# One gated decoder layer on one core: slot attention in one block with its weights loaded ahead, the last expert's down weights in pieces, and token attention written out with scores two batches ahead

## The reference, cut to what matters

```python
x = x + tanh(g_xattn) * cross_attention_and_feed_forward(layernorm(x), ctx)   # not changed
y = layernorm(x)                                                              # [8, 512, 512]
q = broadcast(slot_query)                                                     # [8, 16, 512]
o = q + mha(q, y, y, d_W*, d_b*)                                              # slot attention
h = layernorm(o) * e_ln_g + e_ln_b
u = silu(h @ e_W1 + e_b1) ; g = silu(h @ e_Wg + e_bg)                         # expert e takes slot e
o = o + (u * g) @ e_W2 + e_b2                                                 # 16 experts
x = x + tanh(g_ffn) * mha(y, o, o, c_W*, c_b*)                                # token attention
```

## Time and profile before

| | us |
|---|---|
| median of 3 runs | 2560.3 (2555.49 to 2560.6) |
| the profiled execution | 2563.1 |
| its span | 2561.3 |
| mean granted TensorE clock, share of full speed | 0.929 |
| feed forward ends | 1741.5 |
| slot attention ends | 1934.8 |
| experts end | 2388 |
| last vector step ends | 2556.5 |

### The profile page before, as it was taken

The page is one execution under the profiler, slowest core; times in us unless marked ns, Lnnn a source line. Parts: engine busy times, 40 slices in busy tenths (PEclk is TensorE's granted clock), DMA queues, the critical chain, the costliest instruction groups (busy, mean ns, idle before and its releaser), DMA issues. The chain is left out here.

```text
span 2561.3 us, 29863 instructions
## 1 busy us (share of the span) xinstructions
PE 2231.3 (87%) x11583; PEld 1677.0 (65%) x11583; DVE 959.9 (37%) x1566; ACT 630.7 (25%) x974; POOL 384.4 (15%) x237
## 2 busy tenths in 40 slices
PE   7999999999699999999999999997887535455787
PEld 5677777776588888888888888885773112121576
DVE  7656566655322222222222233334541000000577
ACT  2544455446211111111111111112320000000221
POOL 5443344423100000000000000001210000000022
PEclk9899999999899999999999999997997768777798
DMA  4122210211433333333334353314659999999365
GB/s 148 70 88 88 88 55 34 88 66 34 165 137 137 135 141 137 139 137 136 144 143 143 143 192 124 127 66 159 234 215 394 429 427 429 432 422 424 141 262 213
DMA packets 109716, 466.50 MB, mean 182 GB/s; under 512 B 10850, under 2 KB 12418, under 8 KB 82980
## 3 DMA queue, kind: packets, MB, share of 16 engines
q1 hardware_dynamic: 100372, 406.45, 41.5%
q10 hardware_dynamic: 9264, 58.99, 5.6%
HBM read 381.52 MB, written 83.89 MB: 182 GB/s over the span
## 5 line engine op out<-in xcount | busy, mean ns | idle before, releaser
L1177 ACT ACTIVATE ff_sig<-ff_gate 128x512 f32<-128x512 f32 x128 | 76.5, 598 | 744.7 <-PE ff_a L1137 744.7
L1215 DVE TENSOR_TENSOR u<-ff_sig,ff_a 128x512 f32<-128x512 f32 x128 | 88.0, 687 | 452.3 <-ACT ff_sig L1177 452.3
L1818 PE MATMUL e_down<-e_w,e_ug 128*32 128x512 f32 x512 | 78.0, 765 | 192.0 <-DMA e_w<-in_L_ffn_e_W 186.1
L1137 PE MATMUL ff_gate<-ff_nT_hi,w_hi 128*128 128x512 f32 x512 | 200.3, 391 | 15.1 <-DMA ff_nT_lo<-xnT 15.1
L1137 PE MATMUL ff_gate<-ff_nT_lo,w_hi 128*128 128x512 f32 x512 | 200.0, 391 | 0.0
L1137 PE MATMUL ff_gate<-ff_nT_hi,w_lo 128*128 128x512 f32 x512 | 199.9, 390 | 0.0
L1137 PE MATMUL ff_a<-ff_nT_lo,w_hi 128*128 128x512 f32 x512 | 199.2, 389 | 0.0
L1137 PE MATMUL ff_a<-ff_nT_hi,w_hi 128*128 128x512 f32 x512 | 199.2, 389 | 0.0
L1137 PE MATMUL ff_a<-ff_nT_hi,w_lo 128*128 128x512 f32 x512 | 199.2, 389 | 0.0
L1151 PE MATMUL ff_down<-w_hi,u_hi 128*128 128x512 f32 x512 | 199.2, 389 | 0.0
L1151 PE MATMUL ff_down<-w_lo,u_hi 128*128 128x512 f32 x512 | 199.2, 389 | 0.0
(11 more groups left out here) (365 smaller groups left out, 4457.5 us busy)
## 6 DMA issues: line engine op xcount, KB each, us to landing
e_w<-in_L_ffn_e_W SPq DMA_DIRECT2D x17, 4096.0 KB, 24.4
e_wg<-in_L_ffn_e_Wg SPq DMA_DIRECT2D x16, 4096.0 KB, 34.3
e_w<-in_L_ffn_e_W ACTq DMA_DIRECT2D x14, 4096.0 KB, 49.5
ff_nT_hi<-xnT SPq DMA_DIRECT2D x32, 1024.0 KB, 4.8
ff_nT_lo<-xnT SPq DMA_DIRECT2D x32, 1024.0 KB, 6.8
ff_x<-x SPq DMA_DIRECT2D x32, 1024.0 KB, 8.0
x<-ff_x SPq DMA_DIRECT2D x32, 1024.0 KB, 4.4
ff_raw<-in_L_xattn_Wff SPq DMA_DIRECT2D x36, 256.0 KB, 5.6
```

The source lines that it names most:

```text
L1137: last = nc.tensor.matmul(UP[f % 2][g][:, :], w, m_, start=c == 0, stop=c == 3 * KT - 1)
L1177: nc.scalar.activation(sig[:, f % 2, :], UP[f % 2][1][:, :], ACT.Silu).then_inc(sig_ready, 1)
L1215: nc.vector.tensor_tensor(u32[:, f % 2, :], sig[:, f % 2, :], UP[f % 2][0][:, :], ALU.mult).then_inc(u_ready, 1)
L1818: last = nc.tensor.matmul(YB[q * QW:(q + 1) * QW, :], ug[:, j * Q + q, :], w2[i][:, q * J + j, :], start=j == 0, stop=j == J - 1)
```

## The change

The slot stage becomes one block in which every batch is written out. The order on PE becomes: turn y of b, turn z of b-2, turn the probabilities of b-1, scores of b, sums of b-1. q is made with Wq as the stationary side, 16 columns at a time, into columns, so it isn't turned; A is made of q itself, on four row groups of PE (64 instructions of 16 columns), and q_diag serves the shift alone. The slot queries and column biases, and the first rows of x, are loaded at the end of feed forward; the 17 small rows are loaded behind the store of yT and of batch 0. The value and output products follow in the same block.

```diff
+                        load_slot(sp, 0)
                     with sp.Fori(0, PAIRS - 1) as pair:
                         step(q, pair, pair + 1)
+                    if q == Q - 1:
+                        load_slot(sp, 1)
...
+                for c in range(KT):
+                    for k in range(KT):
+                        last = nc.tensor.matmul(G[5][:, c * NS:(c + 1) * NS], wq[:, k, c * P:(c + 1) * P], sqT[:, k, :], start=k == 0, stop=k == KT - 1)
...
+                for c in range(KT):
+                    for k in range(KT):
+                        for g in range(CH):
+                            rows = slice(g * SD, (g + 1) * SD)
+                            at = (k * KT + c) * NS
+                            last = nc.tensor.matmul(G[g][:, at:at + NS], wkT[rows, c, k * P:(k + 1) * P], qT[rows, c, :], start=True, stop=True)
...
-                with pe.Fori(1, B) as b:
+                for b in range(B):
                     turn_rows(b)
-                    turn_probs(b)
+                    if b >= 2:
+                        turn_sums(b - 2)
+                    if b >= 1:
+                        turn_probs(b - 1)
                     score(b)
-                    sums(b, b - 1)
-                pe.drain().then_inc(g_ready, U_P)
-                turn_probs(B)
-                sums(B, B - 1)
+                    if b >= 1:
+                        sums(b - 1)
+                turn_sums(B - 2)
+                turn_probs(B - 1)
+                sums(B - 1)
+                turn_sums(B - 1)
```

```diff
                 sp.wait_ge(g_ready, E - 1)
+                sp.dma_start(lent[:, 0, :, :], c_weight("q")).then_inc(wq_in, 16)
...
+                sp.wait_ge(last_w2_in[Q - 2], 16)
+                sp.dma_start(lent[:, 1, :, :], c_weight("k")).then_inc(wk_in, 16)
...
                 def finish(e, i):
-                    shrink(e, i)
+                    pe.wait_ge(wq_in, 16)
+                    for c in range(KT):
+                        for k in range(KT):
+                            last = nc.tensor.transpose(WB[c][:, k * P:(k + 1) * P], lent[:, 0, k, c * P:(c + 1) * P], ident[:, :])
...
+                    for q in range(Q):
+                        pe.wait_ge(last_w2_in[q], 16)
+                        for j in range(J):
+                            last = nc.tensor.matmul(YB[q * QW:(q + 1) * QW, :], ug[:, j * Q + q, :], w2[i][:, q * J + j, :], start=j == 0, stop=j == J - 1)
+                    last.then_inc(down_ready, 1)
                     add_parts(e)
```

```diff
+                            if first:
+                                nc.tensor.matmul(bank[at:at + CH * NS, :], first_head[0:1, :], bo, start=False, stop=True)
...
+                for b in range(3):
+                    values(b)
+                pe.wait_ge(w_free, dve_done["wk", KT - 1, CH - 1])
+                scores(0)
+                for b in range(3, 5):
+                    values(b)
+                scores(1)
+                for b in range(5, B):
+                    values(b)
+                for b in range(B - 2):
+                    turn(b)
+                    scores(b + 2)
+                    sums(b)
+                turn(B - 2)
+                turn(B - 1)
+                sums(B - 2)
+                sums(B - 1)
```

998 lines of the change are left out of this document (532 added, 466 removed).

## The result

The changed kernel took 2532.2 us (median of 4 runs, 2528.0 to 2536.3), the kernel before 2559.3 in the same comparison: a ratio of 0.9897, 95% interval 0.9874 to 0.9919, so 1.0% faster, 27 us. The forecast was 2523 with a range of 2505 to 2541. The profiled execution took 2528.0 us, its span 2526.2; before, it was 2563.1 and 2561.3, a difference of 35.1.

What follows compares the result with a forecast made beforehand. TensorE paces slot attention, the weight stream the experts; token attention is mixed. Gains of 21.4 (slots) and 16.1 (token stage, expert's 4.4 loss paid) make 37.5 us: 2525.6 profiled, 2523 median; own range 2513 to 2532, 8-in-10 range 2505 to 2541.

Steps and rivals of the forecast that it cites:

- Entry to batch 1: Slot stage up to batch 1's scores: quicker q and A, earlier yT store; gain 6 us, from 3 to 9.
- Six regular batches: Slot stage: turning z a batch later removes most of two TensorE waits; gain 11.2 us, from 6 to 12.1.
- The end of the slot stage: Last sums in the loop to the wv product: 16.9 us becomes about 12.7; gain 4.2, from 2 to 5.
- Rival C: Weight stream does not pass the slot gain on, being paced by something that does not move; 2544 us, chance 0.07.
- The last expert: Last down product, piece by piece, runs serially in 14.5 us; token stage starts 4.4 us later, with Wq turned.
- Rival A: Narrow products run abreast after all, last down product 3.6 to 6 us, stage ends 9 us sooner; 2514, chance 0.17.
- Token tables: Start of token attention: values 2.9 us a batch; ends at 2461.5 as before, with one more batch of scores done.
- Token batches: Token attention: every batch takes 12.2 us of TensorE, as GpSimd's bo addition no longer stretches VectorE; later ones took up to 15.
- Rival B: Scores ahead bring little in token attention, since VectorE is the bound; 2533 us, chance 0.18.
- The end: Token attention's last turns, sums and addition end at 2542.6, before 2556.5; a store in pieces leaves 2.6 us instead of 4.8.
- Rival D: Slower than before: straight-line programs must be fetched by DMA engines the weight stream holds; 2556 or 2589 us, chance 0.05.

Runs made afterwards that it cites:

- e1: Changed kernel, but ScalarE casts yn_hi of a slot batch behind the four casts of its turned rows instead of ahead of them; 2522.2 us, ratio 0.9857.
- e8: Changed kernel, but Wk, Wv and Wo of token attention are issued right behind Wq, without waiting for piece 2; 2528.7 us in one run.
- e7: Changed kernel without the product that adds bo; GpSimd adds bo to the rows of x for every batch; 2533.1 us, ratio 0.9890.
- e6: Changed kernel, but scores in token attention are made one batch ahead instead of two; 2524.3 us, ratio 0.9857.
- e4: Changed kernel, but three of batch 6's sums precede batch 7's turns, and batch 7's low parts precede the last two additions; 2523.2 us, ratio 0.9862.

## Why the prediction came out as it did

**In sum.** 2532.2 lies in the range and 9 us above the forecast, just over the forecast's own range (to 2532). For the profiled execution 2525.6 was forecast and 2528.0 measured, and that agreement is partly luck: the slot stage gave 9.3 us less than forecast and the token stage 2.4 less, the last expert cost 4.8 less, and 4.4 came from ahead of the change.

**Entry to batch 1: right.** Forecast 6; from the first slot product to the scores of batch 1 it was 44.6 us before and 39.8 after, 4.8. y turns were to start 5 us earlier and did 6.0; A was to take 6 and took 7.02, at the lower clock; the store went first, 5.5 us behind the start of the turns (6 forecast). What came last was ScalarE's cast of y and the casts behind it (wait of 3.70 us), as the text had it.

**Six regular batches: wrong, and the largest miss.** Forecast 11.2, measured 2.6 in five periods of 16.24 instead of 16.77, and nothing between the scores of 1 and of 2. The step that failed is "ScalarE no longer waits for the sums before yn_hi". It waits for the sums two batches back, and these are the ones that end right before the turns of y, in the new order as in the old. Turning z earlier had hidden this cast; without it the cast stands on the path. e1 shows it by moving the cast: 14.89, where the forecast had 14.9.

**The end of the slot stage: right.** Forecast 4.2; from the scores of batch 7 to the value product it was 28.0 us before (from 1888.76 to the row of 1916.78 in the earlier trace rows), 24.2 after, 3.8 less. What follows it took 0.8 less. The stage gave 12.1 instead of 21.4 us, and all of it was handed on: the experts took 452.5 and 452.4 us. Rival C is out.

**The last expert: the mechanism half right, the size wrong.** 14.5 us forecast for the last product, 8.86 measured. The 0.45 us for which a record holds its group is 0.43; what failed is "neighbours share a group, so 32 x 0.45", since two groups run abreast even in this order. Nor does "By it the product is serial" follow from tiles that can run at once: the next group in the program is a different tile. Rival A (3.6 us) was as far off on the other side. A loss of 4.4 us was forecast, and the start of token attention came 0.4 us nearer to the first expert product. That TensorE would wait for no piece was right. The last piece was to land 2.5 us earlier and did land 2.1 earlier (442.5 us after the first expert product, 444.6 before), but not for the reason given: with the loads back in their order (e8) it is 443.1, and other executions scatter by more than that.

**Token tables: right, in part by luck.** From the start of the token stage to the turns of batch 1, 68.9 us forecast (2392.6 to 2461.5) and 68.9 measured (2371.16 to 2440.02), with 2.86 us a batch of values against 2.9. Two errors cancel: the values began 17.4 us behind the start of the stage, where the forecast had 19.4 (to 2412), and from there it took 51.4 us instead of 49.5. And 2.5 us for a low clock stood in the sum; it cost 1.7 in this execution, and up to 7 us more in others. Before, the granted clock over this stage was 0.82, now 0.98: how much of the stage's gain is the waits removed, and how much the clock that fell for a shorter time, no run separates.

**Token batches: right.** 12.2 us a batch forecast, 12.10 measured five times, and no operation of VectorE over 0.75 us there. Rival B is out: VectorE is busy 55.4 of 60.5 us and holds nobody up. The row on VectorE and GpSimd was read rightly: e7 brings the stretched operations back, with batches of 12.9 and 14.9 us, where before there were 13.0 and 14.5.

**The end: 3.1 us too short.** From the turns of batch 6 to the last addition 20.1 us forecast, 23.2 measured. The wait for the last probabilities was foreseen (6.2 us to the end of the turns, measured 6.3); the wait of 1.53 us for the low parts, that stand behind four additions on VectorE, was not, and the two sums took 13.6 us instead of 12.2, since the clock stayed at its lower level for 6.8 us. That the last turns cost that much because scores are two ahead was in the text, and not drawn as a conclusion: e6 and e4 show that it is the change's own loss.

**Rival D** (code to be fetched): nothing in the profiles looks like it, and no run tests it. **The median** is 4 us above the profiled execution; the differences ahead of the slots (4.5 us) and in the tables (7 us) are of that size.

## What to carry to other kernels

When a step is moved off one engine's path, ask what another engine did behind its cover: here a cast of 1.90 us on ScalarE, free as long as TensorE turned z, took the place of the wait that was removed. Of an order that goes through column groups one by one, count the records of the fullest group in a short stretch, and neither all records nor none. And where work is made further ahead, look at the last iteration, which has nothing to put in its place.

## What the runs showed of the hardware that was not expected

A down record (128 x 512, 32 columns) holds its column group for 0.43 us; 32 of them took 8.86 us with one group after the other, 6.64 with two abreast and 3.64 with four. Records of the next group start while those of the last still wait, so even the first order ran two abreast between its first four and its last four records. A product of one row by 64 columns kept its neighbours from running beside it: it adds 1.14 us to a batch of values (2.86 against 1.72 in e7, which has none), one of 128 rows 0.85 (2.57). SP's issues took 9.76 and 10.91 us in the weight stream of e8, each of them holding what stood behind it on SP. And the same products ran at clocks of 0.93 and 0.59 in two executions with the same work ahead of them.
